# A PSUM bank of its own for pair 7's projection, and a new order of every queue behind the last token sums

## What is computed

```python
W = weight * mask[None]                      # (16, 5000, 128)
h = einsum('bg,egp->bep', x, W) + bias       # 64 samples, 16 tokens of 128
n = layernorm(h)
cq, ckv = layernorm(n @ W_dq), layernorm(n @ W_dkv)
Q, K, V = cq @ W_uq, (ckv @ W_ukv)[:, :128], (ckv @ W_ukv)[:, 128:]   # plus rotary parts
h = h + softmax(mask(q k^T * scale)) v @ W_o.T                        # 8 heads, 16 positions
f = layernorm(h)
top 2 of sigmoid(f @ gate_w.T); y_e = (silu(f_e @ w1) * (f_e @ w3)) @ w2   per expert
h = h + 2.5 * sum of the two weighted y_e + shared expert(f)
```

## Time and profile before

| | |
|---|---|
| time, median of 3 runs | 250.8 us (248.49 to 253.65) |
| span of the profiled execution | 258.9 us |
| time of the profiled execution | no other figure than its span is given |
| busy share of the span | PE 72%, DVE 59%, POOL 56%, ACT 32% |
| end of pair 7's sums | about 160.7 us into the span |

### The profile page before, as it was taken

The page is one execution under the profiler, slowest core; times in us unless marked ns, Lnnn a source line. Parts: engine busy times, 40 slices in busy tenths (PEclk is TensorE's granted clock), DMA queues, the critical chain, the costliest instruction groups (busy, mean ns, idle before and its releaser), DMA issues.

```text
span 258.9 us, 6074 instructions
## 1 busy us (share of the span) xinstructions
PE 187.3 (72%) x2479; PEld 154.5 (60%) x2479; DVE 152.3 (59%) x366; ACT 82.7 (32%) x245; POOL 146.2 (56%) x117
## 2 busy tenths in 40 slices
PE   0067967388899796994992997589888799619810
PEld 0067856267789585892991884368667677218410
DVE  0034364956778789689579557697896173001291
ACT  2005100032343432412411342356887342023500
POOL 3336499079989599986877673101516414730270
PEclk9999999779999999797798699657999999967975
DMA  7999999999999999999999995980013292310332
GB/s 256 236 385 420 372 417 329 418 417 417 416 421 424 416 421 413 422 404 391 297 213 232 206 148 85 293 233 5 0 38 109 70 279 60 93 32 21 103 95 52
DMA packets 32981, 65.11 MB, mean 251 GB/s; under 512 B 2874, under 2 KB 25367, under 8 KB 32375
## 3 DMA queue, kind: packets, MB, share of 16 engines
q1 hardware_dynamic: 31416, 59.47, 69.7%
q10 hardware_dynamic: 576, 3.26, 3.0%
q0 software_dynamic: 960, 1.97, 2.8%
HBM read 56.96 MB, written 7.73 MB: 250 GB/s over the span
## 4 chain that ended last, share of the span: by engine, by line
PE 37%; DMA 16%; DVE 16%; SPq 8%; ACT 5%; another core or an unknown queue 5%; POOL 4%; issue 4%; POOLq 1%; DVEq 0%; ACTq 0%
DMA ring<-in_L_tok_weight_dram 15%; PE bank L840 12%; PE bank L1000 4%; SPq L360 4%; PE bank L1030 4%; DVE ring L1220 3%; DVE bank L1250 3%; POOL ring L464 2%; DVE prod L1241 2%; PE bank L1014 2%; SPq L366 2%; PE bank L974 2%; PE bank L883 1%; PE bank L903 1%
## 5 line engine op out<-in xcount | busy, mean ns | idle before, releaser
L464 POOL TENSOR_TENSOR ring<-ring,mask 128x896 f32<-128x896 f32 (+1 forms) x48 | 92.1, 1945 | 18.4 <-DMA ring<-in_L_tok_weight_dram 18.4
L840 PE MATMUL bank<-ring,xT 128*64 128x128 f32 x1248 | 85.4, 295 | 10.6 <-DVE ring L1220 6.6
L840 PEld LDWEIGHTS bank<-ring,xT 128*64 128x64 f32 x1248 | 77.1, 149 | 16.1 <-DVE ring L1220 8.1
L1220 DVE TENSOR_TENSOR ring<-ring,bank 128x1024 f32<-128x1024 f32 (+1 forms) x45 | 45.7, 1048 | 34.7 <-DMA ring<-in_L_tok_weight_dram 34.6
L453 POOL TENSOR_TENSOR rstd<-mv,half 128x1 f32<-128x1 f32 (+1 forms) x24 | 14.3, 603 | 38.3 <-DVE mv L1228 22.8
L531 POOL DMA_INDIRECT ring<-expert_outputs,slot_index x16 | 16.1, 1007 | 26.6 <-DMA expert_outputs<-ring 22.3
L1000 PE MATMUL bank<-w,ring 128*64 128x128 f32 (+1 forms) x256 | 17.0, 322 | 8.0 <-ACT ring L692 5.7
L1000 PEld LDWEIGHTS bank<-w,ring 128*64 128x64 f32 (+1 forms) x256 | 12.9, 146 | 11.4 <-ACT ring L692 6.5
L506 POOL TENSOR_TENSOR mask<-ring,mask 128x256 f32<-128x256 f32 x8 | 7.5, 938 | 17.6 <-ACT ring L701 14.4
L821 PE MATMUL bank<-cst,w 64*128 64x64 f32 x39 | 5.3, 328 | 16.0 <-DMA w<-in_x_dram 15.4
L484 POOL DMA_INDIRECT expert_inputs<-xf,slot_index x14 | 14.3, 1022 | 4.1 <-issue 3.3
(11 more groups left out here) (151 smaller groups left out, 301.8 us busy)
## 6 DMA issues: line engine op xcount, KB each, us to landing
ring<-in_L_tok_weight_dram SPq DMA_DIRECT2D x48, 832.0 KB, 12.6
expert_inputs<-w ACTq DMA_DIRECT2D x3, 1024.0 KB, 9.9
ring<-expert_inputs SPq DMA_DIRECT2D x6, 512.0 KB, 5.4
expert_outputs<-ring SPq DMA_DIRECT2D x12, 256.0 KB
mask<-in_L_tok_mask_dram SPq DMA_DIRECT2D x3, 832.0 KB, 16.1
w<-in_x_dram SPq DMA_DIRECT2D x1, 1250.0 KB, 13.5
w2p<-in_L_ffn_w_dram SPq DMA_DIRECT2D x1, 1024.0 KB
xT<-masks_dram SPq DMA_DIRECT2D x1, 1024.0 KB, 7.9
```

The source lines that it names most:

```text
L464: pool.tensor_tensor(unit(j, q, SPLIT(q // 2), UC), unit(j, q, SPLIT(q // 2), UC), mask[:, (m + SPLIT(q // 2)) * D:(m + UC) * D], ALU.mult ...
L840: last = pe.matmul(bank[0][64 * par:64 * par + 64, 0:D], xT[:, (UC * t + c) * B:(UC * t + c + 1) * B], unit(j, 2 * t + par, c, c + 1), sta ...
L1220: dve.tensor_tensor(both(j, t, a, b), both(j, t, a, b), m.rearrange("p (u f) -> p u f", u=1).to_broadcast([P, 2, (b - a) * D]), ALU.mult). ...
```

## The change

Three things are changed. Pair 7's projection steps (`turn_xn` to `heads_v`) use bank 7 in place of bank 3 (`P_BANK`), so `turn_xn(7)` no longer waits for `heads_v(6)`; `up(1)` goes from bank 5 to bank 3 and waits for `heads_v(6)`; `down(0)`, which uses bank 7, waits for `heads_v(7)` in place of `turn_mid(8)`, and `sum_scores(7)` (bank 5) no longer waits for `silu(1)`. The lists of PE, ACT, DVE and POOL behind the last sums are in another order. Nothing is added to the arithmetic or taken from it.

```diff
 def U_BANK(g):
-    return 5 if g == 1 else 1 if g < GROUPS1 else (1, 5)[g % 2]
+    return 3 if g == 1 else 1 if g < GROUPS1 else (1, 5)[g % 2]
+def P_BANK(j):
+    return 7 if j == NCH - 1 else 3
...
             def turn_xn(j):
                 pe.wait_ge(s_xn, j + 1)
-                if j >= 1:
+                if 1 <= j < NCH - 1:
                     pe.wait_ge(s_kv, 2 * j)
...
-                pe.transpose(bank[3][:, 0:P], xn, ident).then_inc(s_xnT, 1)
+                pe.transpose(bank[P_BANK(j)][:, 0:P], xn, ident).then_inc(s_xnT, 1)
...
+                if g == 1:
+                    pe.wait_ge(s_kv, 2 * (NCH - 1))
...
-                if g == GROUPS1:
-                    pe.wait_ge(s_kv, 2 * NCH)
...
                 if g == 0:
                     pe.wait_ge(s_w2, 16 * 4)
+                    pe.wait_ge(s_kv, 2 * NCH)
...
             def sum_scores(j):
...
-                if j == NCH - 1:
-                    dve.wait_ge(s_sil, 2)
...
             sum_heads(k)
             choose(j)
             multiply_keys(l)
+            add_attended(k)
             sum_scores(l)
             less_max(l)
-            add_attended(k)
+            place(j)
             weigh_values(l)
-            place(j)
             sum_heads(l)
```

More of the change, by code:

```diff
@@ L754, in _ @@
             act.activation(warm[:], half[:, 0:1], ACT.Exp)
+            copy_midT(1)
+            norm_xf(k)
             copy_xsT(5)
-            copy_midT(1)
+            copy_y(0)
+            copy_xfT(k)
             probs(l)
             copy_midT(2)
-            norm_xf(k)
-            copy_y(0)
             silu(4)
@@ L763, in _ @@
             copy_midT(3)
+            silu(5)
             copy_xsT(6)
-            copy_xfT(k)
-            silu(5)
             copy_y(2)
+            copy_midT(4)
             silu(6)
+            copy_oT(l)
             copy_y(3)
-            copy_midT(4)
-            copy_oT(l)
             copy_midT(5)
+            norm_xf(l)
             copy_y(4)
-            norm_xf(l)
             copy_xsT(7)
@@ L1054, in _ @@
             qkv(k)
+            turn_xn(l)
             turn_o(j)
+            project(l)
             values(k)
             attend(j)
-            turn_xn(l)
             turn_xs(0)
-            project(l)
+            turn_qk(l)
             turn_xs(1)
+            qkv(l)
+            up(0)
+            values(l)
             turn_xs(2)
-            up(0)
+            turn_xf(j)
             up(1)
+            gate(j)
             turn_xs(3)
-            turn_qk(l)
-            turn_xf(j)
-            turn_xs(4)
-            qkv(l)
-            gate(j)
             turn_o(k)
-            values(l)
             up(2)
@@ L1075, in _ @@
             turn_mid(0)
+            turn_xs(4)
             up(3)
-            turn_xs(5)
+            rank_tokens(j)
             turn_mid(1)
             down(0)
+            turn_xs(5)
             turn_mid(2)
-            turn_xs(6)
-            rank_tokens(j)
-            up(4)
             turn_xf(k)
             down(1)
+            up(4)
+            gate(k)
             turn_mid(3)
+            down(2)
             up(5)
-            down(2)
-            gate(k)
+            turn_xs(6)
+            turn_mid(4)
+            down(3)
             up(6)
-            down(3)
-            rank_tokens(k)
-            turn_mid(4)
             turn_o(l)
@@ L1096, in _ @@
             attend(l)
+            down(4)
+            rank_tokens(k)
             turn_mid(6)
-            down(4)
             turn_xs(7)
+            turn_xf(l)
             down(5)
-            turn_xf(l)
+            gate(l)
             up(7)
-            gate(l)
             down(6)
```

72 lines of the change are left out of this document (37 added, 35 removed).

## The result

The changed kernel takes 257.86 us (median of 4 runs, 257.05 to 258.75), the kernel before in the same comparison 252.23 (4 runs, 248.49 to 255.14). The ratio is 1.0335, with a 95% interval of 1.0249 to 1.0422: slower, by 6.2 to 10.6 us of 250.8. It is taken from undisturbed runs alone and so is not the quotient of the two medians. The forecast was +5.6 us, and its chances put "within 2%" (0.47) a little ahead of "slower" (0.45). The direction came out, the size was too small, what ended the stage was another step than the forecast took, and the likelier class was the wrong one.

What follows compares the result with a forecast made beforehand. PE was taken as nearly full, with down(7) ending the stage; pair 7's lead is lost, and the loop and late scatter(6) move down(7) from 212.24 to 217.9: +5.6, 256.4 us. Range for 8 in 10: 251.3 to 259.8 us.

Steps and rivals of the forecast that it cites:

- Part 1: Pair 7's projection first: keys 5.8 us earlier, but silu(0) at 180.2 and choose(5) take the lead; round one gains nothing.
- Part 2: Round one in the new order: one chain through ACT and PE from silu(0), with up(5) 2.3 us later than before.
- the right loop: Round one: down(2) waits for copy_y(1), up(5) stands behind down(2), copy_y(2) behind silu(5); 3.9 us a group.
- down(2), up(5): 197.9: Round one's chain on PE: down(2) and up(5), at 1.05 us each, end at 197.9 us.
- Some 3.9 us a group: Loop of round one: each group costs the sum of PE's and ACT's steps, 3.9 us.
- Part 3's sum: End of pairs 6 and 7: late rank_tokens(6) and scatter(6), 8.3 us to turn_xs(8), down(7) at 217.9 against 212.24: +5.6 us.
- some 3 us of its work take 6: +8.6: Upper bound: half clock behind PE's new waits of about 2 us ahead of turn_xf(7) or turn_xs(8).
- were the load there at once: Lower bound without waiting for round two's slots: PE's own list ends the stage, down(7) at 215.8, +3.6 us.
- rival of a clock that rises sooner: Fewer PE gaps from 167 to 178 bring full clock from about 174: +3.8, 254.6 us; chance 0.15.
- faster rival: Pair 7's products no longer cut up round one, PE closes gaps, at most 4.6 us: 246.2 us; chance 0.11.
- the one that the order does not matter: Same steps, PE nearly full in both orders, waits only change places: 250.8 us; chance 0.08.
- A stage behind copy_y(7) that is shorter than the 46.7 us: Sign of being wrong: the time from copy_y(7) to the end falls below 46.7 us (212.2 to 258.9).

Runs made afterwards that it cites:

- banks and head together: Kernel before with the new banks, the new PE list up to up(3) and the new ACT list up to the table load behind silu(3): 249.09 us, ratio 1.0015.
- the shorter fills: Changed kernel plus useless matmuls: 6 ahead of down(2), 8 ahead of turn_xf(7), 5 ahead of turn_xs(8); 253.63 us, ratio 1.0191 to the kernel before.
- the new head: New lists up to up(3) and silu(3); put with the new banks into the kernel before, old lists behind: 249.09 us, ratio 1.0015.
- the old head: Old lists up to up(3) and silu(3); with old banks and the new lists behind them, against the kernel before: 257.53 us, no ratio given.
- the 2.94 us shown above: Changed kernel plus 12 useless matmuls ahead of down(2) (taking 2.94 us) and 14 ahead of turn_xf(7): 257.18 us, ratio 1.0359 to the kernel before.

## Why the prediction was right and wrong

- **Part 1 was right.** Keys at 177.1 foretold, 176.98 measured; silu(0) 180.2 and 180.44; choose(5) 181 and 181.29; sum_heads(7)'s end 196.9 and 196.92. The lead of pair 7 is taken away where the prediction said, and banks and head together cost nothing that the runs can tell.
- **Part 2 was right up to up(4)** (end 193.2 foretold, 193.59 measured) and named the right loop: taking it back gives back 5.5 to 6 us, putting it in alone costs 3 to 5. It missed what the loop does to PE's clock. "down(2), up(5): 197.9" was 199.94; 1.5 of these 2 us are the half clock of both, behind a wait that the working itself shows. "Some 3.9 us a group" was 5.5 from copy_y(1) to copy_y(2) and 3.6 to copy_y(3).
- **Part 3's sum failed in its size.** "I take 5.6, which rests on scatter(6)'s own 8.3 us" is the step: half clock has no term in it. The order at full clock costs +5.7 us, as the shorter fills show, so the sum was right for a PE that keeps its clock (scatter(6) 0.5 us later and the load 0.6 us shorter than in the working, which cancel); but PE does not keep it. Measured: +8.2. The term that held this, "some 3 us of its work take 6: +8.6", stood only at the end of the range. The prediction named the wait ahead of turn_xf(7) as a risk to the clock; the wait of down(2) for copy_y(1) stands in its part 2 without that risk, and the one ahead of turn_xs(8) did not come.
- **What ends the stage was wrong for the kernel as it ran.** The sum let the slots' load end it. In the changed kernel turn_xs(8) has no wait, PE's list at half clock comes last, and an earlier scatter(6) gives next to nothing (255.99 us). It is the branch that the prediction priced as its lower bound, "were the load there at once": its +3.6 with 1.5 us of half clock at down(2) and up(5) and 2.9 from down(5) to down(6) make +8.0. So that +8.6, 3 us on top of the load's branch, came near the +8.2 is in part luck. With the clock held the load comes last, at 7.73 us behind scatter(6) for the 8.3 foretold. Those 8.3 were no time of the load: turn_xs(8) at 210.01 has no wait either. In the profiles where it waits for the load, it starts 7.7 to 9.4 us behind scatter(6).
- **The rival of a clock that rises sooner has the wrong sign.** With the new head the first stretch at 0.50 lasted 17.07 us in each of eight profiles; with the old head, without fills, 13.65, 10.24, 10.24 and 17.07. The Trainium skill has the rule that activity releases the clock (TensorE: Matmul & The Clock Gate, Part 1: The HAM clock gate); no run here shows that closer steps of pair 7 release it sooner, and PE was busy in 14.75 of the 17.07 us.
- **The faster rival and the one that the order does not matter fell** with the ratio, 1.0335 with an interval clear of 1; the first named copy_y(1) by 194.0 as its sign, and it started at 195.59.
- **The chances failed by this term.** One third of the forecast's weight was put under +5 and 0.15 on a clock that rises sooner, none on its own to a clock that falls again. A case "half clock behind the new waits, +8.6" would have put "slower" ahead.
- **One of the tests named was no test.** "A stage behind copy_y(7) that is shorter than the 46.7 us", a sign of being wrong, came true (255.9 - 220.4 = 35.5), since 46.7 held a wait that is in that one profile alone.

## What to carry to other kernels

When an order is priced from a profile, a new wait of PE can have two prices: its length, and the half clock at which PE may do what stands behind it; where PE has no slack, the second belongs into the sum, on the branch that PE itself ends, and not into the end of the range. Keep the next group's first product ahead of the last product of the group before, so that the engine between has something to do; three moves of one position each in PE's list cost more here than all that was left of the change without them. And before believing what ends last, undo only that: the late rank and scatter looked like the bound, and taken back alone they gave 1.8 us of 8.2 in the profile and nothing that the runs can tell.

## What the runs showed of the hardware

Behind PE's waits of 1.75 us (PE busy in 1.77 of the 3.50 us around it) and 2.34 us the granted clock was 0.50 for 3.41 and 6.83 us; the second profile of the changed kernel has the same stretches. Not each wait does it: behind one of 1.39 us ahead of up(2) in the changed kernel (183.20) and one of 1.33 us ahead of down(5) in the kernel before (205.28) it stayed at 1.00. The Trainium skill (TensorE: Matmul & The Clock Gate, HAM oscillation — how this bites in real kernels) tells of a loop that loses its clock in each wait for a transfer; the trace agrees that a wait takes the clock, but here the waits are shorter than that page's, and for a copy and a norm of ScalarE. A useless matmul of 128x128 in float32 took 0.24 us in two records (12 in the 2.94 us shown above), and with fills that fit the clock stayed at 1.00 in both places.

Steps that nothing disturbs repeat from run to run to 0.2 us: down(0) starts 24.45 us behind turn_qk(6) in the changed kernel's first profile and 24.62 in its second, and 24.43 to 24.63 in five of its variants.

The wait of 8.77 us in before's round two stays open. In the 11 us from 220.0 PE has 37 matmuls there, beside 8 gathers; in 11 us of the changed kernel's gathers (from 226.26, 9 of them) it has 272. No other profile of this study has such a wait, and no run was made on it; whether it comes from the fetch of instructions, from the gathers' transfers or from elsewhere was not tried.
